# Splitting the weighing of a quad of heads by key tiles in the two cross-attentions of a decoder kernel

## The reference

```python
q = split_heads(query, W_q)
k = split_heads(key, W_k)
v = split_heads(value, W_v)
scores = jnp.einsum('bqhd,bkhd->bhqk', q, k) / np.sqrt(hd)
scores = jnp.where(kmask, scores, NEG)
attn = jax.nn.softmax(scores, axis=-1)
out = jnp.einsum('bhqk,bkhd->bqhd', attn, v).reshape(B, S, D)
return out @ W_o.T
...
scores = scores + attn_mask[None, None, :, :]
scores = jnp.where(key_padding_mask[:, None, None, :], -jnp.inf, scores)
```

## Time and profile before

| | |
|---|---|
| runs | 656.75, 657.33, 658.64 us; median 657.33 |
| profiled execution | 661.11 us, span 659.4 us |
| busy | PE 533.6 us (81%), DVE 455.0 (69%), ACT 264.9 (40%), POOL 139.1 (21%) |
| L681 + L728 (scores, shifted scores), both layers | 512 records each, 79.8 and 82.0 us |
| L743 (weighing), both layers | 512 records, 34.3 us |
| chain that ended last | PE 62%, DVE 28%, ACT 4%, issue 3% |

### The profile page before, as it was taken

The page is one execution under the profiler, slowest core; times in us unless marked ns, Lnnn a source line. Parts: engine busy times, 40 slices in busy tenths (PEclk is TensorE's granted clock), DMA queues, the critical chain, the costliest instruction groups (busy, mean ns, idle before and its releaser), DMA issues.

```text
span 659.4 us, 8927 instructions
## 1 busy us (share of the span) xinstructions
PE 533.6 (81%) x3166; PEld 305.2 (46%) x3170; DVE 455.0 (69%) x1177; ACT 264.9 (40%) x452; POOL 139.1 (21%) x102
## 2 busy tenths in 40 slices
PE   4888589999969999999999853655564899999633
PEld 3344366666526666666666510122121555555312
DVE  6379845777265536766646458999996458889785
ACT  3532025555534314324324225555530244444642
POOL 6226000000000000030000005899992100000010
PEclk9789778999988889999999975678887799999955
DMA  4000070000010000000000000000001000000000
GB/s 121 0 4 1 0 224 1 2 1 2 1 40 1 0 0 1 1 0 5 1 0 1 0 1 0 0 0 0 1 0 40 0 1 2 1 3 1 1 4 29
DMA packets 10095, 8.20 MB, mean 12 GB/s; under 512 B 1634, under 2 KB 9124, under 8 KB 10052
## 3 DMA queue, kind: packets, MB, share of 16 engines
q1 hardware_dynamic: 10052, 7.64, 4.1%
HBM read 6.98 MB, written 0.52 MB: 11 GB/s over the span
## 4 chain that ended last, share of the span: by engine, by line
PE 62%; DVE 28%; ACT 4%; issue 3%; POOL 2%; DMA 1%; SPq 0%; DVEq 0%; ACTq 0%; POOLq 0%
PE PS L1064 17%; PE PS L1075 9%; PE PS L681 8%; DVE VA L1515 6%; DVE PS L1502 5%; PE PS L743 4%; PE PS L668 3%; DVE PS L1508 3%; PE PS L728 3%; PE PS L719 2%; PE PS L436 2%; PE PS L700 2%; PE PS L753 1%; PE PS L340 1%; DVE SCR L923 1%
## 5 line engine op out<-in xcount | busy, mean ns | idle before, releaser
L1064 PE MATMUL PS<-XNT,KSA 128*128 128x512 f32 x256 | 122.5, 616 | 2.8 <-DVE E L1269 2.0
L878 ACT ACTIVATE E<-PS 128x512 f32<-128x512 f32 x128 | 71.2, 596 | 68.7 <-PE PS L728 42.9
L1269 DVE TENSOR_TENSOR E<-E,PS 128x512 f32<-128x512 f32 x64 | 43.9, 687 | 61.2 <-ACT E L1122 60.8
L1122 ACT ACTIVATE E<-PS 128x512 f32<-128x512 f32 x64 | 38.1, 597 | 111.4 <-PE PS L1064 109.0
L728 PE MATMUL PS<-QM,KP 32*128 32x256 f32 x512 | 82.0, 403 | 0.8 <-ACT E L878 0.8
L681 PE MATMUL PS<-KP,QP 32*128 32x256 f32 x512 | 79.8, 407 | 1.7 <-DVE MXT L923 0.9
L1075 PEld LDWEIGHTS PS<-KSA,E 128*128 128x128 f32 x512 | 64.3, 197 | 18.0 <-issue 17.0
L1064 PEld LDWEIGHTS PS<-XNT,KSA 128*128 128x128 f32 x256 | 46.2, 194 | 46.3 <-issue 42.3
L1075 PE MATMUL PS<-KSA,E 128*128 128x128 f32 x512 | 64.1, 280 | 1.3 <-DVE XN L1260 1.3
L681 PEld LDWEIGHTS PS<-KP,QP 32*128 32x128 f32 x512 | 52.3, 187 | 22.4 <-issue 10.2
L923 DVE CUSTOM_DVE_ANT_0 SCR<-PS,KSA 128x256 f32<-128x256 f32 x128 | 46.5, 420 | 23.3 <-PE PS L681 22.2
(11 more groups left out here) (269 smaller groups left out, 824.8 us busy)
## 6 DMA issues: line engine op xcount, KB each, us to landing
KSA<-in_w SPq DMA_DIRECT2D x2, 1024.0 KB, 7.0
X<-in_x SPq DMA_DIRECT2D x1, 512.0 KB, 4.3
SCR<-in_ctxT SPq DMA_DIRECT2D x1, 512.0 KB, 5.8
SCR<-in_fside SPq DMA_DIRECT2D x1, 512.0 KB, 4.6
out_x<-X SPq DMA_DIRECT2D x8, 64.0 KB, 1.5
wx<-in_w_x SPq DMA_DIRECT2D x1, 384.0 KB, 6.6
wself<-in_w_self SPq DMA_DIRECT2D x1, 256.0 KB, 7.2
KSA<-in_w1T SPq DMA_DIRECT2D x1, 256.0 KB, 10.5
```

The source lines that it names most:

```text
L878: act.activation(slot(m, j), weight_bank(m, j), ACT.Exp).then_inc(sig("exps"), 1)
L1064: ins = pe.matmul(bank(2 * (g % 3) + o), w[:, e, c * P:(c + 1) * P], XNT[:, tokens_of(p)], start=True, stop=True)
L1122: act.activation(E6[:, 4 + g % 2, :], bank(2 * (g % 3)), ACT.Silu).then_inc(sig("silu"), 1)
L1269: dve.tensor_tensor(E6[:, g % 4, :], E6[:, 4 + g % 2, :], bank(2 * (g % 3) + 1), ALU.mult)\
```

## The change

`weigh` gets the key tile as a second argument. Its four matmuls of the first key tile, with all the waits of the weighing, are issued between the two pairs of the round, behind `turn_max`; the four of the second key tile stay where the weighing was, behind the second pair. Both layers run through the same code. No instruction is added or removed.

```diff
-            def weigh(m):
+            def weigh(m, kt):
                 b, g = where(m)
-                pe.wait_ge(sig("exps"), I0 + HG * (m + 1))
-                if m == 0:
-                    pe.wait_ge(sig("queries"), L * B + 4)
-                if m % 2 == 0 and m:
-                    pe.wait_ge(sig("o_taken"), L * QUADS // 2 + m // 2)
-                for kt in range(QT):
-                    for i in range(HG):
+                if kt == 0:
+                    pe.wait_ge(sig("exps"), I0 + HG * (m + 1))
+                    if m == 0:
+                        pe.wait_ge(sig("queries"), L * B + 4)
+                    if m % 2 == 0 and m:
+                        pe.wait_ge(sig("o_taken"), L * QUADS // 2 + m // 2)
+                for i in range(HG):
...
-                ins.then_inc(sig("weighed"), 1)
+                if kt == QT - 1:
+                    ins.then_inc(sig("weighed"), 1)
...
                 if k - 1 < QUADS:
                     turn_max(k - 1)
+                if k > LAG:
+                    weigh(k - LAG - 1, 0)
                 pair(k, 2)
                 if k > LAG:
-                    weigh(k - LAG - 1)
+                    weigh(k - LAG - 1, 1)
```

More of the change, by code:

```diff
@@ L731, in shifted_scores @@
                 ins.then_inc(sig("shifted_scores"), 1)
-            def weigh(m):
+            def weigh(m, kt):
                 b, g = where(m)
-                pe.wait_ge(sig("exps"), I0 + HG * (m + 1))
-                if m == 0:
-                    pe.wait_ge(sig("queries"), L * B + 4)
-                if m % 2 == 0 and m:
-                    pe.wait_ge(sig("o_taken"), L * QUADS // 2 + m // 2)
-                for kt in range(QT):
-                    for i in range(HG):
[L742 to L745, removed]
-                ins.then_inc(sig("weighed"), 1)
+                if kt == 0:
[5 more added lines that the diff above has]
+                for i in range(HG):
+                    j = (i + 2) % HG
+                    ins = pe.matmul(bank(6)[rows(i), (g % 2) * S:(g % 2) * S + S], VX[:, QT * b + kt, HG * g + i, :],
+                                    slot(m, j)[:, kt * S:(kt + 1) * S], start=(kt == 0), stop=(kt == QT - 1),
+                                    skip_group_check=True)
+                if kt == QT - 1:
+                    ins.then_inc(sig("weighed"), 1)
             def turn_out(b, q):
```

## The result

The changed kernel takes 660.02 us at the median (16 runs), the kernel before 657.2 us in the same comparison (16 runs): ratio 1.0042, 95% interval 1.0022 to 1.0061, so 1.4 to 4.0 us slower. Forecast were 659.3 us, 1.9 over before, in a range from 656.2 to 661.4.

A forecast was written before the change was run, and what follows sets the result against it. Each stage was taken as a chain of TensorE blocks and their waits. Layer 0's gain of 3.9 us against layer 1's losses of 3.3 (split) and 2.5 (waits) gave +1.9, so 659.3 us, range 656.2 to 661.4.

The forecast's parts named there:

- both layers pull against each other: Rival 1, the forecast itself: layer 0 gains, layer 1 loses; 659.3 us, own range 658.4 to 660.3, chance 0.50.
- The block price: Both layers: half a weighing costs 0.57 us, two halves 1.14 against 1.00 whole, so 0.14 us more a round.
- The recorded 3.3 us: Layer 1, rounds 3 to 16: splitting the weighing loses 0.23 us in each of 14 rounds.
- Rival 5: Both layers: the seam is free, splits cost 0 in layer 0, 0.09 in layer 1; 655.4 us, chance 0.10.
- Layer 0: First half covers the second pair's 0.48 us wait; 3.4 + 0.2 + 0.4 - 0.1 = 3.9 us gained.
- the margin of 0.02 us: Layer 0: second pair starts 0.94 us behind the transposes, just past the latest bank release at 0.92.
- First pairs of rounds 4 to 7: Layer 0: part of the wait comes back in these first pairs, making them some 1.37 us.
- Rival 4: Layer 0 gives only half, -2 instead of -3.9, as the wait stays in part; 661.1 us, chance 0.10.
- rounds 7 to 16: Layer 0: wait of 0.48 us saved less 0.14 for the split, 0.34 us a round, 3.4 us in all.
- Layer 1: Split loses 3.3 us, new waits for ScalarE's exponentials and evictions lose 2.5; 5.8 us over before.
- Behind rounds 3 and 5: Layer 1: the next first half waits 0.19 us each for the last exponential, 0.4 us in all.
- Rivals 2 and 3: Layer 1's new waits don't come (656.3 us, chance 0.15), or are 0.15 us longer each (660.7 us, chance 0.15).

## Why the prediction was right

The time lies in the range and the mechanism is the one forecast: both layers pull against each other, the waits that were to go went, and those that were to come came. Some sizes were off both ways and cancelled; that part is luck.

- **The block price.** 0.57 us a half was read off one weighing's starts, and every half of both layers has it, to 0.01 us. So the seam is 0.14 us; behind the transposes of layer 1 it is 0.24 (rounds 8, 10, 12 and 14 became 0.24 to 0.25 us longer). The recorded 3.3 us is a little more than 14 times its 0.23, which is 3.2; measured are 3.4. The Trainium skill's rule (TensorEngine Tiling (Array Packing), Key Properties) that a change of tiling mode drains TensorE agrees in sign; no run here shows what the 0.14 us consist of. The 0.175 us that the Trainium skill gives for the drain of a single matmul (TensorE: Matmul & The Clock Gate, Single matmul latency), taken as an estimate of the seam, are above the 0.14 measured. Rival 5, a free seam, is out.
- **Layer 0.** 3.9 us forecast, 3.9 measured, and alone it gives 4.0 at the median. Second pairs are 1.10 us in every round from 3 to 15, so the margin of 0.02 us was enough. First pairs of rounds 4 to 7 came to 1.39 us (119.80 to 123.79 is round 6 with 0.37, 0.57, 1.10, 0.57 and the rest), forecast 1.37. Rival 4 is out. The terms met less well than the sum: rounds 7 to 16 gave 3.6 us, not 3.4, mostly because the second pairs before were not all alike (1.65 us in rounds 11 and 15, 1.49 in round 16); rounds 17 and 18 gave 0.36, not 0.4; round 3 lost 0.18, not 0.1.
- **Layer 1.** 5.8 forecast, 5.6 measured: the first halves of rounds 5 and 7 wait 0.66 and 0.67, ahead of the transposes behind rounds 9 and 13 TensorE loses 0.56 us where it lost 0.32 before (the first pair there takes 1.66 and 1.42 us, elsewhere 1.10), and the halves behind rounds 8, 10, 12 and 14 wait 0.18, 0.13, 0.18 and 0.14 us for bank 6 (forecast 0.18 each; where it is less the out part is a projection of 0.55 us, counted as 0.49). Behind rounds 3 and 5 the half waited 0.09 us and not 0.19: the exponential that ends at 551.65 releases a matmul at 551.70, 0.05 later, where I had taken the 0.14 of an eviction. That term was too large by 0.2 us in all. Rivals 2 and 3 are out by the same waits: the evictions release TensorE 0.14 to 0.15 us after their end, as counted.
- **What stays.** Stage by stage the change is worth +1.7 us in the profiles; the runs say +2.8 with an interval that holds it. That the kernel is slower is shown. Whether by more than the 0.3% (2.0 us) that the forecast took as its bound is not: the interval is 0.22 to 0.61%, and 1.7 us are under the bound. (657.33 + 1.9 is 659.2; the 659.3 on record changes nothing.) A forecast at the edge of what a measurement tells could fall on either side; it fell on "slower", at 0.47.

The forecast missed three things that did not change its sum but did change what the experiments gave: the mask waits for the same exponential as the half; in rounds 3 to 6 a second head that is late with nothing ahead of it costs more than the wait it came from; and an eviction moved ahead of an exponential makes that exponential late.

## What to carry to other kernels

Work that is put into a wait has a price of its own (here 0.14 us a seam, 28 times) and takes its own waits along. So look at each stage separately: the same line of code saved 3.9 us in the layer whose pair waited and lost 5.6 in the one whose pair didn't. And before an instruction with a wait is moved forward, follow its releaser back to the queue in which it stands: an eviction behind an exponential that waits for a third engine is late for no reason of its own. Moved ahead of it, it must not be late itself: in round 17 it was, and cost 0.3 us.

## What the runs showed of the hardware that was not expected

One early stretch moves all that follows by some 4 us from one execution to another. The windows 16 to 32 us of three profiles, in which the program is the same in all (the kernel before, the changed one, and the split of layer 0 alone):

```profile
16.00:32.00 16.00, 14.50 (x35) 5.95 (x33) 5.63 (x11) 8.51 (x18) 4.79 (x4) 0.79 0.00 0
```

```profile
16.00:32.00 16.00, 14.50 (x35) 5.89 (x33) 5.31 (x10) 8.51 (x18) 4.78 (x4) 0.79 0.00 0
```

```profile
16.00:32.00 16.00, 11.00 (x33) 4.51 (x31) 6.17 (x12) 10.13 (x21) 5.46 (x5) 1.00 0.00 0
```

The granted clock, a mean over its two levels (1.2 and 2.4 GHz), is 0.79 of full speed in the first two and 1.00 in the third. The transposes of round 3 in layer 0 then stand at 107.73, 107.86 and 104.00 us. All ten profiles go this way: six have 0.79 to 0.86 in this stretch and the transposes at 107.2 to 107.9 us, four have 1.00 and 103.3 to 104.0: some 4 us decided ahead of the code that was changed, more than the change itself.

In the kernel before, the clock falls to the lower level after 20 us (0.63 in 20 to 24 us, 0.52 in 24 to 28, then 1.00 again), behind 2.50 us of work of TensorE in 16 to 20. The split of layer 0 alone has the same 2.50 us there and keeps 1.00 until 32 us; its clock falls only then (0.57 in 32 to 36 us). Why it falls early in one execution and late in another no run here shows. Nor do the runs show how much of the spread between the times of one kernel comes from it, since one execution of each was profiled.
